# Attention scores in 64-row tiles of the matmul array, instead of from operands stacked by DMA

## The chip, the cores and the metric

The kernel runs on one core of a Trainium2 chip. It is timed in device microseconds (us). The engines are PE (TensorE, matmul; its weight loads are listed apart as PEld), DVE (VectorE), ACT (ScalarE), POOL (GpSimd) and SP (SyncE, here only a DMA queue). Matmul results land in PSUM, eight banks of 128 rows by 512 float32; everything else lies in SBUF.

## The reference

The block is a gated cross-attention followed by a gated top-1 mixture of experts, all in float32: 8 batches of 256 query rows of width 128, 512 context rows each, 16 heads of 64. What matters here is the middle:

```python
xn = _layernorm(x, ln_gamma, ln_beta)            # x is already layer-normed once
q = (xn @ w_q).reshape(B, SQ, NUM_HEADS, DIM_HEAD)
k, v = jnp.split(context @ w_kv, 2, axis=-1)      # then by heads
scores = jnp.einsum('bqhd,bkhd->bhqk', q * SCALE, k)
attn = jax.nn.softmax(scores, axis=-1)
out = jnp.einsum('bhqk,bkhd->bqhd', attn, v).reshape(B, SQ, INNER)
out = (out @ w_out + b_out) * jnp.tanh(gate[0])
```

After it each token picks one of 8 experts by the maximum of its logits, takes a place among at most 160 of that expert, and passes through `relu(x @ w1) @ w2`.

## The kernel before, in words

Every float32 operand of a large product is split in a "hi" and a "lo" part, and a product is three matmuls (hi by hi, lo by hi, hi by lo; `matmul3`). The unit of work is a **pair** of heads: 8 pairs in each of 8 batches, 64 steps in all, which I call slots; `hp` is the pair in the batch, `j` the pair in all. Batches 1 to 6 run in a hardware loop.

In slot `j` the kernel projects keys and queries for pair `j + 4` (`k_project`, `q_project`, PSUM tile `psKQ`); ACT rounds them to hi (`kq_hi`), DVE takes the rest as lo (`kq_lo`), into `HL`, whose upper 64 partitions hold the second head. SP then copies each head's parts by DMA to `ST`, one of four buffers, where one head's hi part lies over its lo part, so that one matmul over all 128 rows forms two of the three products (L400 to L417). A row of minus the maxima rides in the same stack. So a score tile of 128 keys by 256 queries takes two 256-column matmuls (L1106, L1107), 16 a slot, in four steps `c` that alternate between the two banks `psS`.

The maxima for pair `j + 2` come from four 512-column matmuls of hi parts (`max_scores`, L1081, `psM`); DVE reduces them (`row_max`, L802), PE transposes (`max_transpose`, L1091, T below), and ACT writes the row to `ST` (`max_row`). ACT exponentiates the scores to `P32` (L656). DVE and ACT round one head each to float16 (`PHI`; L945, L701), POOL takes the rest (`PLO`, L549). `values` multiplies those of pair `j - 1` with V by 48 matmuls of 65 columns (L1127 to L1129); DVE normalises. One key tile of V is projected a slot (`v_project`, then `v_hi` on ACT and `v_lo` on DVE).

Some slots of a batch carry more: transposes of the attention output and their copy (`o_transposes`, `ot_copy`; hp 0, 1, 4, 6), the output projection (`project`, hp 2), the next context and the token statistics (hp 3), the tokens (`tokens`, hp 4), the choice of experts (`choose`, hp 6) and their places (`place`, hp 7). Each engine runs its list strictly in the order written; semaphores join them. The lists of a slot stand in the `batch` functions.

## Time and profile before

| | |
|---|---|
| median of 3 runs | 570.28 us (567.17 to 572.21) |
| profiled execution | 566.65 us, span 564.9 us |
| mean granted TensorE clock | 0.974 |
| busy share PE / PEld / DVE / ACT / POOL | 89 / 80 / 77 / 68 / 61 % |
| hardware DMA queue, share of 16 engines | 67.2 %, 87.4 MB |

A busy share says how much of the span an engine had an instruction in flight; matmuls overlap their neighbours, so the distance from one start to the next, here called the pitch, tells what one costs in a stream. Of the 87.4 MB, 73.7 are the stacking: 128 transfers of 384 KB and 128 of 192 KB.

### The profile page before, as it was taken

How to read it: one execution, taken by the hardware profiler on the slowest of the kernel's cores; microseconds unless marked ns; L12 is line 12 of the kernel's file. 1: busy time of each engine (PE TensorE's matmuls, PEld its weight loads, DVE VectorE, ACT ScalarE, POOL GpSimd, SP SyncE). 2: the span in 40 equal slices, each digit the busy share in tenths (PEclk: the TensorE clock that was granted, in tenths of full speed). 3: DMA queues.
4: the chain of work that ended last, by engine and by line, in shares of the span. 5: the costliest groups of instructions: out<-in, count | busy, mean ns of one | idle time of the engine just before them, and what ended most of it. 6: DMA issues, size and time to landing. Idle time of an engine off the chain costs nothing.

```text
span 564.9 us, 16275 instructions
## 1 busy us (share of the span) xinstructions
PE 504.8 (89%) x5708; PEld 453.2 (80%) x5708; DVE 437.6 (77%) x814; ACT 382.8 (68%) x671; POOL 343.1 (61%) x210
## 2 busy tenths in 40 slices
PE   4668999999999998999999989999899989986294
PEld 2457889899899887989898979988798979875194
DVE  3579998879987998789878998799869987975112
ACT  3348888768785886688768868687668876872041
POOL 7555579737675666466756666476646664775115
PEclk9879999999999999999999999999999999999599
DMA  7799788957786777577867777577767766850301
GB/s 204 177 238 243 184 212 207 234 116 176 175 204 141 176 167 182 129 175 170 202 146 173 171 174 176 123 174 173 176 143 176 169 141 139 181 148 13 94 10 37
DMA packets 48173, 91.08 MB, mean 161 GB/s; under 512 B 6259, under 2 KB 21027, under 8 KB 48144
## 3 DMA queue, kind: packets, MB, share of 16 engines
q1 hardware_dynamic: 46768, 87.40, 67.2%
q0 software_dynamic: 1376, 3.30, 1.6%
q8 instruction: 18, 0.29, 0.2%
q14 instruction: 11, 0.09, 0.1%
HBM read 10.83 MB, written 5.14 MB: 28 GB/s over the span
## 4 chain that ended last, share of the span: by engine, by line
PE 68%; DVE 11%; issue 7%; ACT 5%; DMA 4%; SPq 2%; POOL 1%; POOLq 0%; DVEq 0%; ACTq 0%
PE psS L1106 9%; PE psM L1081 9%; PE psS L1107 8%; PE psX L1186 4%; PE psO L1127 4%; DVE MX L802 4%; PE psO L1129 4%; PE psKQ L1019 4%; PE psO L1128 4%; PE psKQ L1021 3%; PE psKQ L1020 3%; PE psKQ L1091 2%; PE psX L1139 2%; ACT P L656 2%; PE psX L1020 2%
## 5 line engine op out<-in xcount | busy, mean ns | idle before, releaser
L549 POOL TENSOR_TENSOR PARTS<-P,PARTS 128x1024 f16<-128x1024 f32 x128 | 274.7, 2146 | 163.7 <-ACT PARTS L701 105.4
L656 ACT ACTIVATE P<-psS 128x512 f32<-128x512 f32 x256 | 146.0, 599 | 46.8 <-PE psS L1107 43.2
L802 DVE TENSOR_REDUCE MX<-psM 128x2 f32<-128x1024 f32 x128 | 155.9, 1218 | 11.0 <-PE psM L1081 10.8
L1106 PE MATMUL psS<-ST 128*128 128x256 f32 x512 | 140.8, 302 | 4.0 <-DVE over L896 2.4
L1107 PE MATMUL psS<-ST 128*128 128x256 f32 x512 | 130.2, 282 | 0.0
L1127 PE MATMUL psO<-VH,PARTS 128*128 128x65 f16 x1024 | 106.9, 195 | 2.5 <-POOL PARTS L549 1.6
L1128 PE MATMUL psO<-VL,PARTS 128*128 128x64 f16 x1024 | 105.8, 193 | 0.0
L1129 PE MATMUL psO<-VH,PARTS 128*128 128x65 f16 x1024 | 105.5, 193 | 0.0
L1106 PEld LDWEIGHTS psS<-ST 128*128 128x128 f32 x512 | 97.1, 190 | 9.8 <-issue 6.5
L1107 PEld LDWEIGHTS psS<-ST 128*128 128x128 f32 x512 | 97.5, 190 | 2.4
L1127 PEld LDWEIGHTS psO<-VH,PARTS 128*128 128x128 f16 x1024 | 91.7, 97 | 9.1 <-POOL PARTS L549 2.2
L1129 PEld LDWEIGHTS psO<-VH,PARTS 128*128 128x128 f16 x1024 | 93.6, 97 | 0.0
L1128 PEld LDWEIGHTS psO<-VL,PARTS 128*128 128x128 f16 x1024 | 93.5, 98 | 0.0
L613 ACT ACTIVATE HL<-psKQ 128x768 fp32r<-128x768 f32 x62 | 50.4, 812 | 57.2 <-PE psKQ L1021 53.9
L1081 PE MATMUL psM<-ST 128*128 128x512 f32 x256 | 81.7, 400 | 7.8 <-DMA ST<-HL 5.0
L945 DVE CAST PARTS<-P 128x1024 f16<-128x1024 f32 x64 | 71.3, 1114 | 19.2 <-ACT P L656 16.2
L701 ACT ACTIVATE PARTS<-P 128x1024 f16<-128x1024 f32 x64 | 67.7, 1058 | 5.8
L791 DVE TENSOR_TENSOR VL<-psX,VH 128x512 f16<-128x512 f32 x62 | 42.7, 688 | 20.0 <-ACT VH L631 18.5
L1081 PEld LDWEIGHTS psM<-ST 128*128 128x128 f32 x256 | 43.9, 190 | 14.8 <-issue 4.8
L624 ACT ACTIVATE ST<-psKQ 34x512 fp32r<-34x512 f32 x64 | 38.0, 594 | 14.6 <-PE psKQ L1091 13.3
L783 DVE TENSOR_TENSOR HL<-psKQ,HL 128x512 fp32r<-128x512 f32 x62 | 42.7, 688 | 5.5 <-ACT HL L614 4.3
L631 ACT ACTIVATE VH<-psX 128x512 f16<-128x512 f32 x62 | 36.1, 583 | 2.1 <-PE psX L1021 2.1
(170 smaller groups left out, 850.3 us busy)
## 6 DMA issues: line engine op xcount, KB each, us to landing
ST<-HL SPq DMA_DIRECT2D x128, 384.0 KB, 5.5
ST<-HL SPq DMA_DIRECT2D x128, 192.0 KB, 4.9
ctx_raw<-in_ctx_dram SPq DMA_DIRECT2D x8, 256.0 KB, 4.9
w1s<-in_L_ffn_w_dram SPq DMA_DIRECT2D x8, 256.0 KB, 4.8
w2s<-in_L_ffn_w_dram SPq DMA_DIRECT2D x8, 256.0 KB, 4.5
experts_table<-O POOLq DMA_DIRECT2D x2, 645.0 KB, 6.1
PARTS<-experts_table SPq DMA_DIRECT2D x2, 516.0 KB, 4.2
PARTS<-in_L_xattn_w_kv_dram SPq DMA_DIRECT2D x4, 256.0 KB, 5.1
```

Of the source, the lines that this page charges most:

```text
L549: pool.tensor_tensor(PLO[:, par, h, :], P32[:, h, :], PHI[:, par, h, :], ALU.subtract).then_inc(plo_done, 1)
L613: act.activation(HL[:, hp % 2, H_KHI:H_KHI + KQ], psKQ[:, 0:KQ], ACT.Copy).then_inc(kq_hi_done, 1)
L656: act.activation(P32[:, h, 512 * (c % 2):512 * (c % 2) + 512], psS[c % 2][:], ACT.Exp, scale=SCALE).then_inc(exp_done, 1)
L701: act.activation(PHI[:, hp % 2, 1, :], P32[:, 1, :], ACT.Copy).then_inc(phi1_done, 1)
L802: dve.tensor_reduce(maxima, psM[:], AX.X, ALU.max, negate=True).then_inc(max_done, 1)
L945: dve.tensor_copy(PHI[:, hp % 2, 0, :], P32[:, 0, :]).then_inc(phi0_done, 1)
L1081: last = pe.matmul(psM[:, qt, :], ST[:, buf, h, AQ + P * qt:AQ + P * qt + P], ST[:, buf, h, AK:AQ], start=True, stop=True)
L1106: pe.matmul(dst, ST[:, buf, h, AK + P * kt:AK + P * kt + P], ST[:, buf, h, AQ:STW], start=True, stop=False)
L1107: last = pe.matmul(dst, ST[:, buf, h, BK + P * kt:BK + P * kt + P], ST[:, buf, h, BQ:BK], start=False, stop=True)
L1127: pe.matmul(psO[:, g:g + DH + 1], phi, VH[:, kt, head, 0:DH + 1], start=first_, stop=False)
L1128: pe.matmul(psO[:, g:g + DH], phi, VL[:, kt, head, :], start=False, stop=False)
L1129: last = pe.matmul(psO[:, g:g + DH + 1], plo, VH[:, kt, head, 0:DH + 1], start=False, stop=last_)
```

## The change

Scores and maxima are now made straight from `HL`. The first head's parts lie in partitions 0 to 63, the second's in 64 to 127, and each matmul uses 64 rows of the array; the two heads' matmuls alternate in the program and write different banks. With 64 rows the three products are three matmuls, and minus the maxima come by a fourth, of ones by the row `NM`, 512 columns wide. A slot's scores are thus 4 matmuls of 512 columns and 24 of 256, all of 64 rows, and its maxima 4 of 512 of 64 rows. `ST`, its DMAs and its constants go.

PSUM is dealt anew: `psAB` holds the projection of keys and queries and then scores `c = 0`, `psCD` scores `c = 1` and then the V projection, `psEF` the raw scores for the maxima and then their transposes. The scores of a slot come in two steps of 1024 columns, both heads at once. `AHEAD` falls from 4 to 2, and the maxima are one pair ahead instead of two. `kq_lo` is one instruction of 768 columns instead of two, ACT's extra copy of the queries goes, `P32` and the context parts get a second buffer, the weights' staging gets memory of its own. The batches are written out in the program instead of looped over. In the first batch, two of the x transposes and the statistics of the last ten x tiles are in other slots.

```diff
-    BQ, BK, AK, AQ = 0, SQ, KQ, KQ + SK
-    STW = 2 * KQ
-
-    H_QLO, H_KHI, H_QHI, H_KLO, H_QHI2 = 0, SQ, SQ + SK, 2 * SQ + SK, 2 * KQ
-    HLW = 2 * KQ + SQ
-
-
-    LIFT = 1.875
-    ROW_H, ROW_END = (64, 96), 98
-
-    AHEAD = 4
-    BUFS = AHEAD
+    H_KHI, H_QHI, H_KLO, H_QLO = 0, SK, KQ, KQ + SK
+    HLW = 2 * KQ
+
+
+    LIFT = 7.0
+
+    AHEAD = 2
...
-        P32 = sb("P32", [P, 2, KT * SQ], F32)
+        P32 = sb("P32", [P, 2, 2, KT * SQ], F32)
...
         MX = sb("MX", [P, 2, QT, P], F32)
+        NM = sb("NM", [P, SQ], F32R)
+        ones_r = sb("ones_r", [P, P], F32R)
...
-        psS = [pb(f"psS{i}", [P, 512]) for i in range(2)]
-        psM = pb("psM", [P, QT, 512])
-        psKQ = pb("psKQ", [P, 1024])
+        psAB = pb("psAB", [P, 1024])
+        psCD = pb("psCD", [P, 1024])
+        psEF = pb("psEF", [P, 1024])
         psO = pb("psO", [P, 512])
         psX = pb("psX", [P, 512])
 
@@ -200,9 +195,7 @@
...
-        def kq_banks(j):
-
-            if j in (1, 3):
-                return psS[0][:, 0:SK], psS[1][:, 0:SQ]
-            return psKQ[:, 0:SK], psKQ[:, SK:KQ]
+            return O[:, 1, INNER - n:INNER] if i else P32[:, 0, 0, 0:n]
+
+
+        def kq_bank(j):
+
+            return psCD if j == 1 else psAB
+
+        def score_bank(c):
+
+            return psCD if c else psAB
...
-            def stacks(b, hp):
-
-
-                j = b * PAIRS + hp
-                buf, par = hp % BUFS, hp % 2
-                sp.wait_ge(kq_lo_done, 2 * j + 2)
-                sp.wait_ge(kq_hi_done, 2 * j + 2)
-                if not (is_first(b) and hp < BUFS):
-
-                    sp.wait_ge(score_psum, 4 * j - 4 * (BUFS - 1))
...
-                    if not (is_last(b) and hp + AHEAD >= PAIRS):
-                        stacks(*next_pair(b, hp, AHEAD))
...
                 j = b * PAIRS + hp
-                if not (is_first(b) and hp < 2):
-
-
-                    pe.wait_ge(kq_lo_done, 2 * j - 2 if is_first(b) and hp < AHEAD else 2 * j)
-                if hp == 0:
-                    pe.wait_ge(ctxt_lo_done, b + 1)
+                if j >= AHEAD:
+
+                    pe.wait_ge(exp_done, 2 * (j - AHEAD) + 1)
+                pe.wait_ge(ctxt_lo_done, b + 1)
                 k_cols = slice(INNER + P * hp, INNER + P * hp + P)
-                k_psum, _ = kq_banks(j) if is_first(b) else kq_banks(0)
-                matmul3(k_psum, w_hi[:, k_cols], w_lo[:, k_cols], cT_hi[:], cT_lo[:])
+                matmul3(kq_bank(j)[:, 0:SK], w_hi[:, k_cols], w_lo[:, k_cols], cT_hi[:, b % 2, :], cT_lo[:, b % 2, :])
 
...
-            def max_scores(b, hp, h):
+                matmul3(bank[:], cT_hi[:, b % 2, cs], cT_lo[:, b % 2, cs], w_hi[:, ws], w_lo[:, ws]).then_inc(v_psum, 1)
+
+            def max_scores(b, hp, qt):
+
+
                 j = b * PAIRS + hp
-                buf = hp % BUFS
-                if h == 0:
-                    pe.wait_ge(stack_in[buf], stack_value(b, hp))
-                if not (is_first(b) and hp == 0 and h == 0):
-                    pe.wait_ge(max_done, 2 * j + h)
+                hl = HL[:, hp % 2, :]
+                if qt == 0:
+                    pe.wait_ge(kq_hi_done, j + 1)
+                    if j:
+
+                        pe.wait_ge(mrow_done, j)
+                else:
+                    pe.wait_ge(max_done, 2 * j + 1)
+                for h in range(2):
+                    rows = slice(64 * h, 64 * h + 64)
+                    last = pe.matmul(psEF[:, 512 * h:512 * h + SK], hl[rows, H_QHI + P * qt:H_QHI + P * qt + P],
+                                     hl[rows, H_KHI:H_KHI + SK], start=True, stop=True)
+                last.then_inc(smax_psum, 1)
+
...
+            def scores(b, hp, c):
+
+
                 j = b * PAIRS + hp
-                pe.wait_ge(max_done, 2 * j + 2)
-
-                pe.wait_ge(kq_lo_done, 2 * kq_before)
-                for qt in range(QT):
-                    last = pe.transpose(psKQ[:, KQ + P * qt:KQ + P * qt + P], MX[:, hp % 2, qt, :], ident[:])
-                last.then_inc(mt_psum, 1)
-
-            def scores(b, hp, c):
+                hl = HL[:, hp % 2, :]
+                if c == 0:
+                    pe.wait_ge(mrow_done, j + 1)
+                    pe.wait_ge(kq_lo_done, min(j + 2, B * PAIRS))
+                    if j == 0:
+                        pe.wait_ge(row_consts, 4)
+                    if j + 1 >= B * PAIRS:
+
+                        pe.wait_ge(exp_done, 2 * j - 1)
+                elif j == 0:
+                    pass
+                elif v_group(*back(b, hp, 1)):
+
+                    vb, half, kt = v_group(*back(b, hp, 1))
+                    pe.wait_ge(v_lo_done, vb * 2 * KT + half * KT + kt + 1)
+                else:
+                    pe.wait_ge(exp_done, 2 * j)
+                heads = [(slice(64 * h, 64 * h + 64), score_bank(c)[:, 512 * h:512 * h + 512]) for h in range(2)]
+                for rows, dst in heads:
+                    both = NM[rows, :].unsqueeze(1).to_broadcast([64, 2, SQ])
+                    pe.matmul(dst.rearrange("p (i n) -> p i n", i=2), ones_r[rows, :], both, start=True, stop=False)
+                for i in range(2):
+                    kt = 2 * c + i
+                    for k, q in ((H_KHI, H_QHI), (H_KHI, H_QLO), (H_KLO, H_QHI)):
+                        for rows, dst in heads:
+                            last = pe.matmul(dst[:, SQ * i:SQ * i + SQ], hl[rows, k + P * kt:k + P * kt + P],
+                                             hl[rows, q:q + SQ], start=False, stop=(i == 1 and k == H_KLO))
+                last.then_inc(score_psum, 1)
+
...
+                    if more1:
+                        max_scores(*next_pair(b, hp, 1), 0)
                     scores(b, hp, 0)
                     scores(b, hp, 1)
...
                     if more1:
-                        max_transpose(*next_pair(b, hp, 1), j + AHEAD if ahead else B * PAIRS)
+                        max_scores(*next_pair(b, hp, 1), 1)
...
+                    if j:
+                        values(*back(b, hp, 1))
...
                     if ahead:
+                        if is_first(b) and hp == 2:
+                            pe.wait_ge(w_lo_rest_done, 3)
                         k_project(*next_pair(b, hp, AHEAD))
-                    if more2:
-                        max_scores(*next_pair(b, hp, 2), 0)
-                    if ahead:
                         q_project(*next_pair(b, hp, AHEAD))
+                    if more1:
+                        max_transpose(*next_pair(b, hp, 1))
...
+                    if v_group(b, hp):
+                        if j == 0:
+                            pe.wait_ge(w_lo_rest_done, 3)
+                        v_project(*v_group(b, hp), after_exp=2 * j + 2)
...
-                dve.wait_ge(kq_hi_done, 2 * j + 2)
+                dve.wait_ge(kq_hi_done, j + 1)
                 hl = HL[:, hp % 2, :]
-                k_psum, q_psum = kq_banks(j) if is_first(b) else kq_banks(0)
-                dve.tensor_tensor(hl[:, H_KLO:H_KLO + SK], k_psum,
-                                  hl[:, H_KHI:H_KHI + SK].bitcast(F32), ALU.subtract).then_inc(kq_lo_done, 1)
-                dve.tensor_tensor(hl[:, H_QLO:H_QLO + SQ], q_psum,
-                                  hl[:, H_QHI:H_QHI + SQ].bitcast(F32), ALU.subtract).then_inc(kq_lo_done, 1)
-
-            def v_lo(b, half, kt, bank=psX):
+                dve.tensor_tensor(hl[:, H_KLO:H_KLO + KQ], kq_bank(j)[:, 0:KQ],
...
+                    exps(b, hp, 0)
+                    exps(b, hp, 1)
+                    act.wait_ge(exp_done, 2 * j + 2)
+                    if not (is_first(b) and hp < 2):
+
+                        act.wait_ge(pv_done, j - 1)
+                    act.activation(PHI[:, hp % 2, :, 512:1024], P32[:, hp % 2, :, 512:1024], ACT.Copy)\
+                       .then_inc(phi_done[1], 1)
+                    if not (is_last(b) and hp + AHEAD >= PAIRS):
+                        kq_hi(*next_pair(b, hp, AHEAD))
                     if not (is_last(b) and hp + 1 >= PAIRS):
                         max_row(*next_pair(b, hp, 1))
...
+                    more1 = not (is_last(b) and hp + 1 >= PAIRS)
+                    if more1:
+                        row_max(*next_pair(b, hp, 1), 0)
+                    phi_first(b, hp)
+                    if more1:
+                        row_max(*next_pair(b, hp, 1), 1)
+                    if hp == LOGITS_STEP and not is_first(b):
+
+                        dve.wait_ge(logit_psum, b)
+                    if hp == RANKS_STEP and not is_first(b):
+                        dve.wait_ge(pos_psum, b)
+                    if not (is_first(b) and hp == 0):
+                        normalise_heads(*back(b, hp, 1), is_first(b) and hp == 1)
                     if not (is_last(b) and hp + AHEAD >= PAIRS):
                         kq_lo(*next_pair(b, hp, AHEAD))
```

On PE, first the stretch from the second half of the maxima to the next slot's first scores (`psM` raw scores, `psX` V, `psS` scores), as it was:

```order
L1081 MATMUL psM<-ST 128x512 [waits max_done]
L1081 MATMUL psM<-ST 128x512
L1030 ISA
L1068 REGISTER_ALU [waits ot_done]
L1019 MATMUL psX<-w_hi,cT_hi 128x512 [waits ctxt_lo_done]
L1020 MATMUL psX<-w_lo,cT_hi 128x512
L1021 MATMUL psX<-w_hi,cT_lo 128x512
L1102 ISA [waits mrow_done]
L1106 MATMUL psS<-ST 128x256 [waits exp_done]
L1107 MATMUL psS<-ST 128x256
L1106 MATMUL psS<-ST 128x256
L1107 MATMUL psS<-ST 128x256
```

And the same stretch now, up to the second half of the maxima (V goes to `psCD`, raw scores to `psEF`):

```order
L942 MATMUL psCD<-w_hi,cT_hi 128x512 [waits ctxt_lo_done,exp_done]
L943 MATMUL psCD<-w_lo,cT_hi 128x512
L944 MATMUL psCD<-w_hi,cT_lo 128x512
L1006 MATMUL psEF<-HL 128x512 [waits mrow_done,kq_hi_done]
L1006 MATMUL psEF<-HL 128x512
L1042 MATMUL psAB<-NM,ones_r 128x512 [waits kq_lo_done,mrow_done]
L1042 MATMUL psAB<-NM,ones_r 128x512
L1047 MATMUL psAB<-HL 128x256 x12
L1042 MATMUL psCD<-NM,ones_r 128x512 [waits v_lo_done]
L1042 MATMUL psCD<-NM,ones_r 128x512
L1047 MATMUL psCD<-HL 128x256 x12
L1006 MATMUL psEF<-HL 128x512 [waits max_done]
```

Before, scores waited for the maxima's row and for the exponential that frees their bank. Now the first scores wait for `kq_lo_done`, the lo part of the pair two further, which lies in the same bank, and the second half of the maxima stands in front of everything that follows and waits for DVE.

On DVE, one slot before (`psM` raw scores, `psKQ` keys and queries, `psX` V):

```order
L945 CAST PARTS<-P 128x1024 [waits pv_done]
L796 REGISTER_ALU
L802 TENSOR_REDUCE MX<-psM 128x2 [waits mt_psum,smax_psum]
L780 ISA
L783 TENSOR_TENSOR HL<-psKQ,HL 128x512 [waits kq_hi_done]
L785 TENSOR_TENSOR HL<-psKQ,HL 128x256
L790 REGISTER_ALU
L791 TENSOR_TENSOR VL<-psX,VH 128x512 [waits v_hi_done]
L809 RECIPROCAL rden<-psO 128x4 [waits pv_done]
L813 REGISTER_ALU [waits rden_done]
L817 TENSOR_TENSOR O<-psO,rden 128x2x2x64 [waits ot_psum]
L802 TENSOR_REDUCE MX<-psM 128x2 [waits mt_psum,smax_psum]
```

And one slot now (`psAB` keys and queries, `psCD` V):

```order
L729 TENSOR_REDUCE MX<-psEF 128x2 [waits mt_psum,smax_psum]
L737 CAST PARTS<-P 128x2x512 [waits pv_done,exp_done]
L729 TENSOR_REDUCE MX<-psEF 128x2 [waits mt_psum,smax_psum]
L744 RECIPROCAL rden<-psO 128x4 [waits pv_done]
L752 TENSOR_TENSOR O<-psO,rden 128x2x2x64 [waits ot_psum,rden_done]
L713 TENSOR_TENSOR HL<-psAB,HL 128x768 [waits kq_hi_done]
L719 TENSOR_TENSOR VL<-psCD,VH 128x512 [waits v_hi_done]
L729 TENSOR_REDUCE MX<-psEF 128x2 [waits mt_psum,smax_psum]
```

The two reductions (L729) stood a whole slot ahead of their use; now they are in the slot that uses them, and the first stands behind `v_lo` (L719) of the slot before and whatever else that slot gave DVE at its end.

## Rows read from the trace of the kernel before

**Rows 1.** The page: span, and busy time of each engine.

```profile
span 564.9 us, 16275 instructions
...
PE 504.8 (89%) x5708; PEld 453.2 (80%) x5708; DVE 437.6 (77%) x814; ACT 382.8 (68%) x671; POOL 343.1 (61%) x210
```

**Rows 2.** The page: the chain that ended last, share by engine.

```profile
PE 68%; DVE 11%; issue 7%; ACT 5%; DMA 4%; SPq 2%; POOL 1%; POOLq 0%; DVEq 0%; ACTq 0%
```

**Rows 3.** PE in order of time: start us, duration us, instructions.

```profile
119.68 0.42 PE L1091 MATMUL psKQ<-ident,MX 128*128 128x128 f32 x2
...
282.23 0.42 PE L1091 MATMUL psKQ<-ident,MX 128*128 128x128 f32 x2
...
289.04 0.41 PE L1091 MATMUL psKQ<-ident,MX 128*128 128x128 f32 x2
...
290.82 3.73 PE L1186 MATMUL psX<-wo,OT 128*128 128x128 f32 x32
...
482.04 0.42 PE L1091 MATMUL psKQ<-ident,MX 128*128 128x128 f32 x2
```

**Rows 4.** PE in order of time, within one slot.

```profile
240.36 0.39 PE L1020 MATMUL psKQ<-cT_lo,w_hi 128*128 128x512 f32 x1
240.59 0.39 PE L1021 MATMUL psKQ<-cT_hi,w_lo 128*128 128x512 f32 x1
...
242.81 0.20 PE L1127 MATMUL psO<-VH,PARTS 128*128 128x65 f16 x1
...
243.52 0.20 PE L1129 MATMUL psO<-VH,PARTS 128*128 128x65 f16 x1
243.55 0.36 PE L1106 MATMUL psS<-ST 128*128 128x256 f32 x1
243.75 0.28 PE L1107 MATMUL psS<-ST 128*128 128x256 f32 x1
243.87 0.28 PE L1106 MATMUL psS<-ST 128*128 128x256 f32 x1
```

**Rows 5.** Groups by line: xcount, then busy us, mean ns, idle before.

```profile
L802 DVE TENSOR_REDUCE MX<-psM 128x2 f32<-128x1024 f32 x128 | 155.9, 1218 | 11.0 <-PE psM L1081 10.8
L656 ACT ACTIVATE P<-psS 128x512 f32<-128x512 f32 x256 | 146.0, 599 | 46.8 <-PE psS L1107 43.2
...
L613 ACT ACTIVATE HL<-psKQ 128x768 fp32r<-128x768 f32 x62 | 50.4, 812 | 57.2 <-PE psKQ L1021 53.9
...
L791 DVE TENSOR_TENSOR VL<-psX,VH 128x512 f16<-128x512 f32 x62 | 42.7, 688 | 20.0 <-ACT VH L631 18.5
...
L631 ACT ACTIVATE VH<-psX 128x512 f16<-128x512 f32 x62 | 36.1, 583 | 2.1 <-PE psX L1021 2.1
```

**Rows 6.** ACT in order of time: two exponentials back to back.

```profile
229.42 1.08 ACT L656 ACTIVATE P<-psS 128x512 f32<-128x512 f32 x2
```

**Rows 7.** DVE in order of time: statistics, tokens, choice and places.

```profile
212.86 2.15 DVE L902 TENSOR_TENSOR slot_now<-pos,over 128x2 uint32<-128x2 f32 x1
...
247.20 0.14 DVE L840 COPY mark<-gscale 128x1 f32<-128x1 f32 x1
...
248.38 0.68 DVE L945 CAST PARTS<-P 128x1024 f16<-128x1024 f32 x1
...
254.25 1.58 DVE L853 TENSOR_SCALAR row<-row,mv,rstd 128x128 f32<-128x128 f32 x2
...
265.45 0.16 DVE L864 TENSOR_REDUCE lmax<-psO 128x2 f32<-128x16 f32 x1
...
272.69 0.16 DVE L883 TENSOR_TENSOR rank<-psO,taken 128x16 f32<-128x16 f32 x1
...
274.00 1.23 DVE L802 TENSOR_REDUCE MX<-psM 128x2 f32<-128x1024 f32 x1
```

**Rows 8.** PE's weight loads in order of time: four in a row.

```profile
264.18 0.53 PEld L1154 LDWEIGHTS psO<-gw,tT 128*128 128x128 f32 x4
```

**Rows 9.** PE in order of time: the wait ahead of the first slots.

```profile
22.95 1.05 PE L1081 MATMUL psM<-ST 128*128 128x512 f32 x2 [4.40 <-DMA ST<-HL]
```

More of the change, by code:

```diff
@@ L224, in gated_block @@
         kq_lo_done = sem("kq_lo_done")
-        stack_in = [sem(f"stack_in{i}") for i in range(BUFS)]
         smax_psum = sem("smax_psum")
@@ L231, in gated_block @@
         exp_done = sem("exp_done")
-        phi0_done = sem("phi0_done")
-        phi1_done = sem("phi1_done")
+        phi_done = [sem(f"phi{c}_done") for c in range(2)]
         plo_done = sem("plo_done")
@@ L290, in is_first, with each_batch @@
             return isinstance(b, int) and b == 0
-        def each_batch(eng, body):
-            body(0)
-            with eng.Fori(1, B - 1) as b:
+        def each_batch(body):
+            for b in range(B):
                 body(b)
-            body(B - 1)
-        def stack_value(b, hp):
-            return b * (64 * PAIRS // BUFS) + 64 * (hp // BUFS + 1)
         def v_group(b, hp):
@@ L422, in x1_store @@
                 sp.dma_start(out_b[b], x_now).then_inc(x1_out, 16)
-            for hp in range(AHEAD):
-                stacks(0, hp)
             sp.dma_start(bo[:], b_out.rearrange("(o n) -> o n", o=1).to_broadcast([P, D])).then_inc(bo_in, 16)
@@ L619, in max_row, with v_hi @@
                 act.wait_ge(mt_psum, j + 1)
-                if not (is_first(b) and hp < BUFS):
-                    act.wait_ge(score_psum, 4 * j - 4 * (BUFS - 1))
-                rows = slice(ROW_H[0], ROW_END)
-                act.activation(ST[rows, hp % BUFS, :, BQ:BK],
-                               psKQ[rows, KQ:KQ + SQ].unsqueeze(1).to_broadcast([ROW_END - ROW_H[0], 2, SQ]),
-                               ACT.Copy).then_inc(mrow_done, 1)
-            def v_hi(b, half, kt, bank=psX):
+                act.activation(NM[:], psEF[:, 0:SQ], ACT.Copy).then_inc(mrow_done, 1)
+            def v_hi(b, half, kt, bank=psV):
                 n = b * 2 * KT + half * KT + kt
@@ L707, in batch @@
                         router_exp(b - 1)
-            each_batch(act, batch)
-            ot_copy(B - 1, 3, psS[0])
-            tokt_copy(B - 1, psS[1])
+            each_batch(batch)
+            ot_copy(B - 1, 3, FFN_BANKS[0])
+            tokt_copy(B - 1, FFN_BANKS[1])
             router_exp(B - 1)
@@ L913, in _ @@
             split_w(2)
-            for hp in range(2):
-                kq_lo(0, hp)
-                v_lo(0, 0, hp, V_BANKS[hp])
+            kq_lo(0, 0)
+            dve.wait_ge(row_consts, 1)
+            row_max(0, 0, 0)
+            kq_lo(0, 1)
+            row_max(0, 0, 1)
+            for kt in range(KT):
+                v_lo(0, 0, kt, V_BANKS[kt])
             dve.wait_ge(x_rest_in, 16)
@@ L1316, in rows_out @@
                     s = 2 * i + n
-                    last = pe.transpose(psS[i % 2][:, P * n:P * n + P], yT[:, P * s:P * s + P], ident[:])
+                    last = pe.transpose(FFN_BANKS[i % 2][:, P * n:P * n + P], yT[:, P * s:P * s + P], ident[:])
                 last.then_inc(yrow_psum, 1)
```

368 lines of the change are left out of this document (137 added, 231 removed).

## The prediction, made before the changed kernel ran

> **What bounds the kernel now.** I read the page's busy times first [rows 1]: PE is busy 89% of the span, more than any other. The chain that ended last agrees: 68% of it is PE's [rows 2]. Then PE in order of time, to see what a slot costs. From one maxima transpose to the next, 282.23 to 289.04, an ordinary slot takes 6.81 us; batch 1's first listed transpose (119.68) and batch 7's (482.04) lie six batches apart, so a batch takes 60.4 us [rows 3]. Within a slot the starts follow each other without a hole: a 512-column matmul takes 0.23 us of pitch, a 256-column one 0.12, 24 value matmuls with 23 gaps 0.71, so 0.031 each, and the first float32 matmul after them 0.08 more [rows 4]. PE is fed because work for a pair is made two to four slots ahead. That lead, not PE's work alone, is what the change alters.
>
> **PE's own work.** With the heads side by side at full effect, scores are 2 steps of 0.23 + 6 x 0.12 = 0.95 us, 1.90 a slot against 16 x 0.12 = 1.92 now: no gain. The maxima fall from 4 x 0.23 to 2 x 0.23, a gain of 0.47 a slot, 30 us over 64 slots if PE stayed the bound. Changing between 64 and 128 rows costs something twice a slot, no row shows it. Nothing is the lower end. The upper is 0.3: a matmul lasts 0.28 at a pitch of 0.12, so letting the array run empty exposes 0.16, and a first load and matmul as much again. I take 0.2. Of the page TensorEngine Tiling (Array Packing) in the Trainium skill, the section Key Properties says that changing the tiling mode drains TensorE; by it the lower end would fall away and the sum stay. No row here shows such a change.
>
> **The first loop.** Pair j+2's keys and queries are projected into the bank that the next slot's first scores need. From scores to scores: scores 1.90, second maxima 0.23, mode change 0.2, values 48 x 0.031 + 0.08 = 1.54, keys and queries 3 x 0.23 + 3 x 0.12 = 1.06 and 0.16 until the last has ended [rows 4], `kq_hi` on ACT 0.81 [rows 5], `kq_lo` on DVE. That one is now 768 columns wide; 512 take DVE 0.69 and 768 take ACT 0.81, 1.5 times 0.69 would be 1.03; I take 0.96. Three hand-overs, between nothing and 0.1 each, 0.2 together. Sum **7.06 us**. While kq_hi and kq_lo run, PE has only T, the V projection and the first maxima, about 1.2 us, and then stands still for some 0.8. This eats the 0.47 and more: 7.06 against 6.81.
>
> **The second loop** runs over DVE. The second maxima wait for the first reduction, values, keys and queries stand behind them, and the first reduction stands behind `v_lo`. Reduction 1.22, maxima and mode change 0.43, values 1.54, keys and queries 1.22, kq_hi 0.81, kq_lo 0.96, v_lo 0.69, hand-overs 0.2, less 0.1 for each instruction that starts while the one ahead of it still drains (two of 0.60 take 1.08 together [rows 5, 6]): 6.9, just below the first loop. So all that DVE gets at a slot's end counts nearly in full. In four slots a batch the copy `ot_copy` adds a third way: kq_hi 0.81, the row of maxima (256 columns, 0.35 by those of 512 and 768), ot_copy 0.60 (as wide as an exponential), v_hi 0.58, v_lo 0.69, each less 0.1, and then reduction to queries as before: **7.3**.
>
> **By slot of a batch.** hp 0 and 1: 7.3 each. hp 2: the projection is 3.7 us of PE [rows 3] that fall on PE's own work of about 6.2, with 0.5 of waits for the late v_lo and reduction: 10.4. hp 3: 6.9 plus the context's lo part 0.6 and the statistics, 247.20 to 248.38, 1.2 [rows 7]: 8.7. hp 4: 7.3 plus tokens 1.5: 8.8. hp 5: 7.06 plus copies: 7.4. hp 6: 7.3 plus the choice, five instructions of 0.16 that wait for one another, 0.9: 8.3 with a little cover. hp 7: 6.9 plus places, 272.69 to 274.00, 1.3 or, where its last instruction takes 2.15 instead of 0.16 (212.86, one of five of eight), 3.3; mean 2.5: 9.4. Sum 67.6 against 60.4 (which holds all these extras, mostly covered): **+7.2 a batch, 50 over seven batches**.
>
> The first batch: PE no longer waits 4.40 us for the first stack [rows 9], but two x transposes and the statistics of ten x tiles move into its slots, and these are longer too. I take +5, between -4 and +10. The exponentials, roundings and POOL's part keep their columns, and POOL, at 61%, has room in longer slots. The expert part after the last batch keeps its instructions. The 67% DMA share and ACT's second copy go, worth nothing: neither was waited for in the steady slots.
>
> Sum: +55. The profiled execution took 566.65 us, so 622; the median of the runs shown is 3.6 above it, so I say **625**. Its own range: mode change 0 to 0.3 (-13, +6), hand-overs and kq_lo 0.1 a slot either way (6), first batch (-9, +5): 603 to 642.
>
> **Rivals.**
> *The loads don't run side by side.* Four loads of 128 columns, with matmuls of 8 columns that hide nothing, take 0.53 us for the four, the last 0.19 long: one each 0.113 [rows 8]. Were each of 24 loads of a slot's narrow matmuls to take that in turn, scores are 2.71 + 0.47 = 3.2 instead of 1.9. The first loop becomes 8.3, and only slots that are already longer are spared: 8.3, 8.3, 11.3, 8.8, 8.8, 8.8, 8.4, 9.4, 72.1 a batch, +11.7 x 8: about 664. For it: f32 loads are as dear as 256-column matmuls, and the change has more of them. Against: the heads use different rows. The Trainium skill's page TensorE: Matmul & The Clock Gate, section LDWEIGHTS (loading the stationary operand), says that a load's time follows its columns and not its rows, so halving the rows makes none cheaper; whether two overlap, no row here shows. Chance 0.15.
> *Nothing runs side by side.* Then scores take 4 x 0.23 + 24 x 0.12 = 3.8 and the maxima 0.93 as now; the first loop is 9.2, a batch about 77.5, 17.1 more, and with 8 of them the kernel about 707. Chance 0.08.
> *Faster: PE stays the bound.* The place is kq_hi and kq_lo between the queries and the next scores. If they with their hand-overs took under 1.2 us instead of 2.0, PE's other work would cover them; then a slot is PE's own 6.81 - 0.47 + 0.1, and the kernel about 566.65 - 24, so 546 as a median, if the reductions too come early. For it: 16 busy DMA engines no longer write SBUF, and DVE's cast takes 0.68 at 248.38 [rows 7], when POOL is idle, so an engine's time depends on its neighbours. Against: kq_hi and kq_lo work from PSUM, and to decide it they must shrink by two fifths. Chance 0.08, some of it only part of the way.
> *No net change*: the waits cost just what the maxima save, 0.47 a slot, with DVE's extras covered. Chance 0.05; between this and my forecast lies 0.04.
>
> **How the numbers follow.** The forecast itself has 0.60. The range runs from 590 to 675: it takes in the forecast's own, most of the way down to no change, and the case of loads in turn; outside lie 707 and the fast end, about 0.2. Within 1% is about what a measurement of this kernel can tell from no change. Faster by over 1%: 0.08; within: 0.05; slower: 0.87.
>
> **What would show it.** First, two score matmuls of different heads starting close together, a pair each 0.12 us: else a rival of the loads. Second, on PE a hole of about 0.8 us ahead of the first scores of most slots, released by kq_lo, and one ahead of the second maxima released by the reduction, longest after hp 3, 4, 6 and 7. Third, slots of 7.0 to 7.3 us, hp 2 near 10.4, a batch near 68. PE's busy share should fall though the kernel is longer. I am wrong if PE shows no such holes, or if the batch stays near 60.

## The result: 4.5% slower, half of what was forecast

| | before | after |
|---|---|---|
| median | 570.56 us (567.17 to 572.21, 4 runs) | 595.92 us (594.97 to 596.14, 4 runs) |
| profiled execution, its span | 566.65, 564.9 us | 596.11, 594.1 us |
| one batch, T to T | 60.39 us | 64.53 us |

The ratio is 1.045, interval 1.040 to 1.050. The forecast was 625, between 590 and 675, with 0.87 for slower. Direction and range held; the forecast's 9.6% were twice the real 4.5%.

The page of the changed kernel, span and busy shares, the DMA queue, then the chain that ended last:

```profile
span 594.1 us, 15490 instructions
...
PE 511.3 (86%) x6476; PEld 427.2 (72%) x6476; DVE 394.9 (66%) x750; ACT 349.0 (59%) x477; POOL 326.8 (55%) x208
...
q1 hardware_dynamic: 18096, 11.88, 6.8%
...
PE 56%; DVE 22%; ACT 11%; issue 5%; DMA 2%; POOL 2%; SPq 0%; POOLq 0%; DVEq 0%; ACTq 0%
```

Against [rows 1, 2]: every engine is busy for a smaller share, and in the chain that ended last PE's share fell from 68 to 56%, DVE's rose from 11 to 22% and ACT's from 5 to 11%. No engine is the bound; hand-overs between them are. Groups by line, with idle time before them and its releaser, say which:

```profile
L500 POOL TENSOR_TENSOR PARTS<-P,PARTS 128x1024 f16<-128x1024 f32 x128 | 271.7, 2145 | 178.3 <-DVE PARTS L737 178.2
...
L713 DVE TENSOR_TENSOR HL<-psAB,HL 128x768 fp32r<-128x768 f32 x63 | 60.3, 958 | 84.4 <-ACT HL L555 84.4
...
L555 ACT ACTIVATE HL<-psAB 128x768 fp32r<-128x768 f32 x63 | 51.3, 814 | 82.4 <-PE psAB L944 82.4
...
L1006 PE MATMUL psEF<-HL 64*128 64x512 f32 x256 | 63.3, 487 | 26.8 <-DVE MX L729 21.6
...
L737 DVE CAST PARTS<-P 128x1024 f16<-128x1024 f32 x64 | 47.9, 749 | 14.2 <-ACT P L591 13.8
```

kq_hi waits for the queries and kq_lo for kq_hi, 63 times each: the first loop. The second maxima (L1006) wait 21.6 us for the reduction: the second. kq_lo is 0.96 us as estimated. (The cast's mean of 749 ns is 63 of 0.68 to 0.70 us and one of 4.47, beside two subtractions on POOL in the second slot.) The next view is PE in order of time through a slot of hp 7, from one transpose to the next (8.13 us); a 64-row matmul shows as 64*128:

```profile
286.06 0.38 PE L1015 MATMUL psEF<-ident,MX 128*128 128x128 f32 x2
286.20 0.48 PE L942 MATMUL psCD<-w_hi,cT_hi 128*128 128x512 f32 x1
...
287.49 0.51 PE L1006 MATMUL psEF<-HL 64*128 64x512 f32 x2 [0.34 <-ACT NM L561]
288.21 0.49 PE L1042 MATMUL psAB<-NM,ones_r 64*128 64x512 f32 x2 [0.22 <-DVE HL L713]
288.52 0.90 PE L1047 MATMUL psAB<-HL 64*128 64x256 f32 x12
289.23 0.42 PE L1042 MATMUL psCD<-NM,ones_r 64*128 64x512 f32 x2
...
291.18 0.51 PE L1006 MATMUL psEF<-HL 64*128 64x512 f32 x2 [0.81 <-DVE MX L729]
291.62 0.20 PE L1068 MATMUL psO<-VH,PARTS 128*128 128x65 f16 x1
...
294.19 0.38 PE L1015 MATMUL psEF<-ident,MX 128*128 128x128 f32 x2
```

Twelve narrow matmuls last 0.90 us with 0.28 of the last one's drain in it: 0.62 for 11 gaps, 0.056 each, so 0.113 a pair, as with full overlap. From the first score tile's start to the second's it is 1.02 (288.21 to 289.23), 0.07 over the forecast. The hole ahead of the first scores, released by kq_lo, is there in 54 slots, but of 0.2 us, or 0.5 by the starts (288.21 less 287.49 and 0.23), where 0.8 had been forecast. The hole of 0.81 ahead of the second maxima is released by the reduction. DVE in the same slot (start, duration) shows what held that reduction:

```profile
287.98 0.68 DVE L719 TENSOR_TENSOR VL<-psCD,VH 128x512 f16<-128x512 f32 x1
288.58 0.17 DVE L818 TENSOR_TENSOR rank<-psO,taken 128x16 f32<-128x16 f32 x1
...
289.81 0.16 DVE L837 TENSOR_TENSOR slot_now<-pos,over 128x2 uint32<-128x2 f32 x1
289.90 1.23 DVE L729 TENSOR_REDUCE MX<-psEF 128x2 f32<-128x1024 f32 x1
```

Its maxima were done at 288.00, but v_lo and 12 instructions of `place` stand ahead of it: it starts 1.9 us late. `place` takes 1.3 us here and its last instruction 0.16; in before that one took 1.98 to 2.15 in five of eight batches [rows 7]. POOL at that time, first in before, then in the changed kernel:

```profile
212.85 2.14 POOL L549 TENSOR_TENSOR PARTS<-P,PARTS 128x1024 f16<-128x1024 f32 x1 [1.51 <-ACT PARTS L701]
```
```profile
283.58 4.24 POOL L500 TENSOR_TENSOR PARTS<-P,PARTS 128x1024 f16<-128x1024 f32 x2 [3.66 <-DVE PARTS L737]
290.06 0.19 POOL L485 TENSOR_TENSOR pool_mark<-mhalf 128x1 f32<-128x1 f32 x1 [2.23 <-DVE slot_now L837]
```

In before the last instruction of `place` (212.86 to 215.01) lies beside a subtraction (212.85 to 214.99). In the changed kernel both subtractions have ended at 287.82, ahead of `place`.

Forecast and measured pitch by slot, from the same T rows (batches 1 to 6 agree within 0.02):

| hp | 0 | 1 | 2 | 3 | 4 | 5 | 6 | 7 | batch |
|---|---|---|---|---|---|---|---|---|---|
| forecast | 7.3 | 7.3 | 10.4 | 8.7 | 8.8 | 7.4 | 8.3 | 9.4 | 67.6 |
| after | 7.20 | 7.19 | 10.22 | 8.41 | 7.70 | 7.52 | 8.19 | 8.12 | 64.53 |

### The profile page after: what moved, and what is told of

Its sections match the earlier page's. It is cut to its first block, busy times and chain, and to the rows that moved or that the text cites. A ratio compares the mean times of both kernels' runs of the same rounds, so it can differ in the third digit from the quotient of the medians.

```text
span 594.1 us, 15490 instructions
## 1 busy us (share of the span) xinstructions
PE 511.3 (86%) x6476; PEld 427.2 (72%) x6476; DVE 394.9 (66%) x750; ACT 349.0 (59%) x477; POOL 326.8 (55%) x208
## 4 chain that ended last, share of the span: by engine, by line
PE 56%; DVE 22%; ACT 11%; issue 5%; DMA 2%; POOL 2%; SPq 0%; POOLq 0%; DVEq 0%; ACTq 0%
PE psO L1068 7%; DVE HL L713 6%; ACT HL L555 6%; DVE MX L729 6%; PE psO L1070 5%; PE psO L1069 5%; PE psAB L942 5%; PE psEF L1006 4%; PE psX L1127 4%; PE psCD L1047 4%; PE psAB L944 4%; PE psAB L943 4%; DVE VL L719 4%; PE psAB L1047 3%; PE psAB L1042 2%
## 5 line engine op out<-in xcount | busy, mean ns | idle before, releaser
L729 DVE TENSOR_REDUCE MX<-psEF 128x2 f32<-128x1024 f32 x128 | 156.2, 1221 | 0.5 <-PE psEF L1006 0.5
L713 DVE TENSOR_TENSOR HL<-psAB,HL 128x768 fp32r<-128x768 f32 x63 | 60.3, 958 | 84.4 <-ACT HL L555 84.4
L591 ACT ACTIVATE P<-psAB,lift 128x1024 f32<-128x1024 f32 x64 | 71.3, 1113 | 66.4 <-PE psAB L1047 66.4
L555 ACT ACTIVATE HL<-psAB 128x768 fp32r<-128x768 f32 x63 | 51.3, 814 | 82.4 <-PE psAB L944 82.4
L1006 PE MATMUL psEF<-HL 64*128 64x512 f32 x256 | 63.3, 487 | 26.8 <-DVE MX L729 21.6
L591 ACT ACTIVATE P<-psCD,lift 128x1024 f32<-128x1024 f32 x64 | 70.9, 1108 | 11.3 <-PE psCD L1047 10.3
L1006 PEld LDWEIGHTS psEF<-HL 64*128 64x128 f32 x256 | 24.8, 184 | 57.2 <-DVE MX L729 27.5
L1047 PEld LDWEIGHTS psCD<-HL 64*128 64x128 f32 x768 | 59.0, 188 | 1.1
L1047 PEld LDWEIGHTS psAB<-HL 64*128 64x128 f32 x768 | 57.8, 185 | 1.6
L1047 PE MATMUL psCD<-HL 64*128 64x256 f32 x768 | 58.4, 281 | 0.0
L1047 PE MATMUL psAB<-HL 64*128 64x256 f32 x768 | 57.7, 278 | 0.0
L719 DVE TENSOR_TENSOR VL<-psCD,VH 128x512 f16<-128x512 f32 x60 | 41.3, 689 | 14.6 <-ACT VH L566 14.1
```

What stands on the lines that cost most here:

```text
L555: act.activation(HL[:, hp % 2, H_KHI:H_KHI + KQ], kq_bank(j)[:, 0:KQ], ACT.Copy).then_inc(kq_hi_done, 1)
L591: act.activation(P32[:, hp % 2, :, 512 * c:512 * c + 512], score_bank(c)[:].rearrange("p (h n) -> p h n", h=2), ACT.Exp, bias=lift[:, 0:1] ...
L713: dve.tensor_tensor(hl[:, H_KLO:H_KLO + KQ], kq_bank(j)[:, 0:KQ], hl[:, H_KHI:H_KHI + KQ].bitcast(F32), ALU.subtract).then_inc(kq_lo_done, 1)
L719: dve.tensor_tensor(VL[:, kt, 8 * half:8 * half + 8, :], bank[:].rearrange("p (h d) -> p h d", d=DH), VH[:, kt, 8 * half:8 * half + 8, 0:D ...
L729: dve.tensor_reduce(maxima, psEF2, AX.X, ALU.max, negate=True).then_inc(max_done, 1)
L1006: last = pe.matmul(psEF[:, 512 * h:512 * h + SK], hl[rows, H_QHI + P * qt:H_QHI + P * qt + P], hl[rows, H_KHI:H_KHI + SK], start=True, sto ...
```

## The experiments

Each kernel is the changed one with the edit shown, in the main lines of it. Where a kernel ran only once there is no interval; the verdict then rests on its slots and batches, which repeat from batch to batch within 0.05 us unless the text says otherwise.

### Which path: the projections earlier, or the second maxima later

```diff
 # kq_early: PE
                     if more1:
                         max_scores(*next_pair(b, hp, 1), 1)
+                    if ahead:
+                        k_project(*next_pair(b, hp, AHEAD))
+                        q_project(*next_pair(b, hp, AHEAD))
                     if j:
                         values(*back(b, hp, 1))
 # kq_hi ahead of ACT's rounding of the second half, kq_lo ahead of normalise_heads
```

> The changed kernel, but the keys and queries of pair j+2 are projected right after the second maxima, ahead of the values; ACT rounds them ahead of its half of the exponentials, DVE takes their low part ahead of the normalisation. Theory 1 (the path queries, kq_hi, kq_lo, next scores sets the slot): values of 1.5 us now cover kq_hi and kq_lo; the hole ahead of the first scores goes, a slot falls from 7.2 to about 6.5 and the batch from 64.5 to 59 or less, so 545 to 562 us, faster than the kernel before. Rival (the reductions set the slot: second maxima behind the first reduction): the hole only moves to the second maxima, batch stays within 1.5 us of 64.5, time 584 to 600.

Measured: 590.63 us median, 1.034 of before (1.030 to 1.038). The batch is 64.1, slots 7.14. Missed: the first loop's wait ahead of the scores is gone, but the slot is only 0.06 shorter, because the path V projection, v_hi, v_lo, first reduction, second maxima, which the projections now stand behind, is as long. PE's wait for the reduction grew from 21.6 to 28.2 us. The rival's numbers came true (584 to 600 us, a batch within 1.5 of 64.5).

```diff
 # m1_late: PE
-                    if more1:
-                        max_scores(*next_pair(b, hp, 1), 1)
                     if j:
                         values(*back(b, hp, 1))
+                    if more1:
+                        max_scores(*next_pair(b, hp, 1), 1)
```

> The changed kernel, but the second maxima stand behind the values instead of ahead of them. Nothing on PE waits for the first reduction any more until the values are done. Theory 1 (the path over kq_hi and kq_lo sets most slots, the reduction only those after DVE's extra work): the long slots hp 3, 4, 6 and 7 give back 0.3 to 0.7 us each, but the second reduction and with it the transpose end later; batch 62.5 to 64, time 580 to 592. Rival (the reductions set every slot): 0.5 us or more in every slot, batch 60 or less, time below 567.

Measured: 601.32 us, 1.053 (1.049 to 1.057), slower than the change as it is. Both theories missed. Three of the four long slots fell, as theory 1 said, though by other amounts: hp 3 and 4 from 8.41 and 7.70 to 7.37 and 7.51, hp 6 to 7.64; but the ordinary slots rose from 7.2 to 7.5, hp 7 to 8.9 and hp 2 to 10.65, and the batch stayed at 64.6. The transpose's loads now wait 25.5 us in all for the second reduction, which starts a pass of values later. Each move takes one of two nearly equal paths away and leaves or feeds the other.

### What made DVE's operations long before, and short now

After, tokens take 342 ns each and slot_now 161; before, 803 and 1381 in the mean of the groups. Two things differ: where POOL's subtractions lie, and the DMA traffic. One experiment for each (its waits are left out here):

```diff
 # pool_extra: POOL, behind its subtractions
+                    if hp in (TOK_STEP, RANKS_STEP) and not is_first(b):
+                        pool.tensor_tensor(pool_out[:], wraw[:, 0:1024]..., wraw[:, 1024:2048]..., ALU.subtract)
 # dma_back: SP, in every slot from batch 1 on
+                    for h in range(2):
+                        src = wraw[64 * h:64 * h + 64, 0:2 * KQ]
+                        sp.dma_start(sink[0:64, h, :], src)
+                        sp.dma_start(sink[64:128, h, 0:KQ], src[:, 0:KQ])
```

> The changed kernel with one more subtraction of 128x1024 on POOL, into a tile of its own, behind POOL's work of slots hp 4 and hp 7 of every batch but the first; nothing waits for it. It is there to run beside DVE's tokens (two of 0.34 us) and places. Theory A (a busy POOL is what makes DVE's operations on SBUF alone long): tokens rise from 0.60 for the two to 1.2 or more, the last instruction of places or one of its neighbours from 0.16 to 1 or more, in most batches, and the time rises by 6 to 15 us. Theory B (they were long before because of the stacks' DMA traffic): tokens and places keep 0.60 and 0.16, time within 3 us of 596.

> The changed kernel with the DMA traffic of the kernel before put back: in every slot from batch 1 on, four transfers from SBUF to SBUF with the shapes of the stacks (1.18 MB a slot), from a tile that nobody writes to one that nobody reads; nothing waits for them but the next ones. Theory A (POOL makes the DVE operations long): tokens 0.60 for two, slot_now 0.16, cast 0.69 as without, time within 3 us of 596. Theory B (the DMA traffic makes them long): tokens 1.2 or more for two, cast 1.0 or more, slot_now 1 or more, batch longer by 2 us and more, time above 608.

Measured: pool_extra 621.3 us, dma_back 600.5. The second moved 75.6 MB on the queue, 54.5% of the 16 engines' span (before: 87.4 MB, 67.2%), and the means of these groups are those of the changed kernel to the nanosecond:

```profile
L752 DVE CAST PARTS<-P 128x1024 f16<-128x1024 f32 x64 | 47.9, 749 | 14.2 <-ACT P L606 13.7
...
L803 DVE TENSOR_SCALAR row<-row,mv,rstd 128x128 f32<-128x128 f32 x16 | 4.8, 342 | 0.8 <-POOL rstd L490 0.8
...
L852 DVE TENSOR_TENSOR slot_now<-pos,over 128x2 uint32<-128x2 f32 x8 | 1.3, 161 | 0.3
```

So theory B is out. Its time is 4.6 us over the change as it is, more than the 3 expected, and lies in single slots: one hp 3 of 10.40 instead of 8.41, where PE waits 2.10 us for the next context to land, and four of hp 7 of 8.33 to 8.75, which I did not trace further. In pool_extra, DVE and then POOL around one `tokens`:

```profile
338.46 0.96 DVE L725 TENSOR_TENSOR HL<-psAB,HL 128x768 fp32r<-128x768 f32 x1 [1.34 <-ACT HL L567]
339.72 0.69 DVE L731 TENSOR_TENSOR VL<-psCD,VH 128x512 f16<-128x512 f32 x1 [0.29 <-ACT VH L578]
340.32 1.66 DVE L800 TENSOR_SCALAR row<-row,mv,rstd 128x128 f32<-128x128 f32 x2
341.90 1.21 DVE L741 TENSOR_REDUCE MX<-psEF 128x2 f32<-128x1024 f32 x1
```
```profile
335.04 4.25 POOL L504 TENSOR_TENSOR PARTS<-P,PARTS 128x1024 f16<-128x1024 f32 x2 [1.01 <-DVE PARTS L749]
339.24 2.41 POOL L511 TENSOR_TENSOR pool_out<-wraw 128x1024 f16<-128x1024 f32 x1
```

kq_lo and v_lo, which read PSUM, run beside POOL at 0.96 and 0.69, as ever. Of the tokens, SBUF to SBUF, the first ends with POOL's subtraction (341.65) and the second behind it: 1.66 for the two instead of 0.60. By the starts and ends of all such rows: 0.60 with POOL idle, 1.64 and more in 7 of 7 beside it. In `place` it is not the last instruction that grows but one of its neighbours, the third:

```profile
296.39 1.35 DVE L834 TENSOR_TENSOR rank_hot<-rank,hot_padded 128x16 f32<-128x16 f32 x1
```

The cast takes 0.68 to 0.70 in 63 of 64 cases, here and in the changed kernel, all of them with POOL's subtractions ended or not yet begun; in before 51 of 64 casts overlap one, and their median is 1.27, up to 1.81. Theory A holds for the durations; its time was forecast 6 to 15 us up and is 25 up. The Trainium skill's page SBUF — State Buffer, section SBUF: two separate sides, says that VectorE and GpSimd share one pair of ports as an exclusive lock, which VectorE asks for in a two-port mode or with two SBUF inputs, and that it is the only contention among engines; by that rule the trace agrees.

The batch of pool_extra is 68.3 us and its time 621 us, close to the 67.6 and 625 forecast. hp 4 rose by 1.06 to 8.76 (8.8 forecast), the tokens' own. hp 7 rose by 2.7 to 10.8, past the forecast's 9.4, though `place` grew only by 1.2. Most of what came on top is the clock, in PE's stretches behind the hole (columns: window, us, busy of PE, PEld, DVE, ACT and POOL, granted clock, DMA share, GB/s):

```profile
297.00:299.90 2.90, 0.92 (x16) 0.72 (x12) 2.87 (x12) 2.87 (x3) 1.32 (x3) 1.00 0.00 0
299.90:302.00 2.10, 2.10 (x32) 1.78 (x33) 1.75 (x2) 0.30 (x1) 1.79 (x3) 0.56 0.18 67
302.00:304.00 2.00, 2.00 (x25) 1.87 (x23) 0.61 (x2) 0.00 (x0) 2.00 (x2) 0.61 0.21 74
```

PE stood still for 1.98 us ahead of 299.89, then the granted clock was 0.56 and 0.61 in these windows; the stretch 300.2 to 303.5 alone has 0.50, the lower of the two levels (1.2 of 2.4 GHz). There value matmuls take 0.055 apiece instead of 0.031. So the batch of pool_extra comes near its forecast in part by luck: the clock's loss in hp 7 was in no forecast. In the changed kernel the hole of that slot is 0.81 us and the clock stays 1.00.

### What DVE's extra work costs at a slot's end

```diff
 # extras_late: DVE
                         row_max(*next_pair(b, hp, 1), 0)
+                    if hp == MOMENTS_STEP + 1 and not is_first(b):
+                        token_moments(b - 1)
+                    if hp == TOK_STEP + 1 and not is_first(b):
+                        tokens(b - 1)
                     phi_first(b, hp)
```

> The changed kernel, with nothing moved but token_moments and tokens on DVE: they stand behind the first reduction of the next slot, ahead of the cast, instead of ahead of the reduction. It measures what the reduction's path charges for DVE's extra work. Theory 1 (in the slots of hp 3 and hp 4 the first reduction and with it the second maxima wait for them in full): their pitch falls from 8.41 and 7.70 to 7.6 to 7.8 and 7.1 to 7.3, batch 1.0 to 1.4 us shorter, time 585 to 589. Rival (the reduction is not what these slots wait for): batch within 0.3 us of 64.5, time 592 to 598.

Measured: 586.38 us, batch 63.0, hp 3 at 7.40 and hp 4 at 7.19, all else as it was. Theory 1, a little more than asked for: 1.5 us a batch instead of 1.0 to 1.4, 10 us for four lines moved. The second loop, with all of DVE's extras in it, was described rightly.

### Are the heads side by side, and who sees to it

```diff
 # heads_apart: three matmuls of head 0, three of head 1, again for the other 256 columns
 # heads_far: all seven of head 0, then all seven of head 1
 # one_half: both heads from rows 0 to 63
-                heads = [(slice(64 * h, 64 * h + 64), score_bank(c)[...]) for h in range(2)]
+                heads = [(slice(0, 64), score_bank(c)[...]) for h in range(2)]
```

> The changed kernel, with the score matmuls of each 256-column half in the order three of head 0, then three of head 1, instead of head by head in turn. Work and shapes are the same. Theory 1 (matmuls on different halves of the rows run side by side only where neighbours in the row differ in head; those of one head take 0.113 each in turn): twelve matmuls take 9 steps of 0.113 instead of 6, that is 1.02 instead of 0.68 in pitch, 0.68 a slot more, nearly all on the path: batch 69 to 70, time 628 to 640. Rival (PE takes matmuls of the other head early, past a waiting one): no difference, within 4 us of 596.

> The changed kernel, with all seven matmuls of head 0 for a score tile ahead of all seven of head 1. In turns of three the order made no difference. Theory 1 (PE goes on to a matmul of the other half past waiting ones, at least six of them): no difference, within 4 us of 596, the twelve narrow matmuls still start 0.057 apart. Rival (it looks past three or so): the seven of one head run for the most part alone, 0.23 and 6 x 0.113 = 0.91 of pitch a head, up to 0.7 more for each of two tiles a slot, and the time between 610 and 690.

> The changed kernel, with the scores of both heads computed from rows 0 to 63, so that head 1's are those of head 0: the same number and shapes of matmuls, all on one half of the array's rows. Theory 1 (two matmuls on different halves share a step of 0.113, those of one half take one each): scores take 2 x (0.47 + 1.36) = 3.6 in pitch instead of 1.9, all on the path, batch 14 us longer, time 690 to 710. Rival (a matmul of 64 rows takes half a step by itself and nothing runs side by side): no difference, within 4 us of 596.

Measured: 595.46, 617.48 and 691.61 us. one_half bears out that the halves matter: an ordinary slot takes 8.9 instead of 7.2, as 3.6 for 1.9 asks, though slots with waits absorb a part, so that the batch is 74.5, 10 longer and not 14; three slots of 11.95 with a lower clock bring the time to where it was expected. Twelve narrow matmuls now last 1.60 us:

```profile
296.31 0.70 PE L1042 MATMUL psAB<-NM,ones_r 64*128 64x512 f32 x2 [0.21 <-DVE HL L713]
296.85 1.60 PE L1047 MATMUL psAB<-HL 64*128 64x256 f32 x12
```

That is (1.60 - 0.28) / 11 = 0.12 each; on two halves it is 0.056. So the overlap is real and comes from the halves. heads_apart missed: no difference, where I had expected 9 steps for 6. heads_far came out as its rival said (PE looks past three or so), 0.62 a slot and a time between 610 and 690. PE in order of time there, first score tile:

```profile
290.70 0.46 PE L1042 MATMUL psAB<-NM,ones_r 64*128 64x512 f32 x1 [0.20 <-DVE HL L713]
291.01 0.51 PE L1046 MATMUL psAB<-HL 64*128 64x256 f32 x3
291.25 0.50 PE L1042 MATMUL psAB<-NM,ones_r 64*128 64x512 f32 x1
291.36 0.74 PE L1046 MATMUL psAB<-HL 64*128 64x256 f32 x6
```

In the program head 1's wide matmul (the second L1042) stands behind six narrow ones of head 0; it starts at 291.25 when three of them have. Here, then, PE takes a matmul for the free half past three waiting ones, not past six. The alternation that the change writes out is safe but not needed to that depth. The Trainium skill's page TensorE: Matmul & The Clock Gate, section The mechanism, says that matmuls start and end strictly in program order; this trace differs, and the measurement decides.

### What a change of rows costs

```diff
 # switch64 (switch128: rows 0:128), in values
                 for h in range(2):
+                    if h == 1:
+                        pe.matmul(psO[:, 320:328], ones_r[0:64, :], ones_r[0:64, 0:8], start=True, stop=True)
```

> The changed kernel, with one matmul of 64 rows and 8 columns, into a corner of psO that nobody reads, between the two heads' values in every slot: two more changes between 64 and 128 rows a slot. The changed kernel's rows show 0.43 from the last maxima to the first value matmul, 0.20 above its pitch, and 0.09 from the projections to the maxima. Theory 1 (the change of mode is what costs that): 0.3 to 0.5 us a slot between the heads, nearly all on the path, time 614 to 628. Rival (the 0.20 belongs to the maxima's last matmul and not to the change): 0.1 a slot or less, time below 604.

> The same as switch64, with the added matmul of 8 columns on 128 rows, so that nothing changes between 64 and 128 rows there. It is the control: what is left of the 0.31 us a slot that switch64 added is the matmul's own, with its change from half precision to float32 and back. Theory 1 (the change of mode is dear): 0.1 to 0.15 a slot, batch 65.3 to 65.7, time 602 to 606. Rival (most of it is the float32 matmul among half-precision ones): 0.25 or more a slot, batch 66.5 or more, time 611 to 616.

Measured: 615.18 and 604.03 us; batches 67.0 and 65.5. Eight slots each: +0.31 and +0.12 a slot. The control takes the float32 matmul's own 0.12 away, and by the batches (67.0 less 65.5, over eight) 0.18 is left for the two changes of rows; for the two of the changed kernel's own slot 0.2 had been taken. The Trainium skill's page TensorEngine Tiling (Array Packing), section Key Properties, says that changing the mode drains TensorE; the trace agrees in that two changes cost 0.18 us, and it shows no drain by itself.

### The order that the two paths ask for

Both must run beside the values. `reorder` puts PE's slot as: maxima, scores, second maxima, keys and queries, V projection, transpose, the batch's extra work, values; the V projections one slot later in the table (else v_hi would overwrite values still being read); ACT kq_hi, row of maxima, v_hi, then its rounding; DVE kq_lo, v_lo, then the normalisation. `reorder2` adds extras_late, `reorder3` moves choose and place too:

```diff
 # reorder3: DVE
                         row_max(*next_pair(b, hp, 1), 0)
+                    if hp == LOGITS_STEP + 1 and not is_first(b):
+                        choose(b - 1)
+                    if hp == 0 and b >= 2:
+                        place(b - 2)
                     phi_first(b, hp)
```

> The changed kernel in another order. PE, in a slot: maxima, scores, second maxima, keys and queries of pair j+2, V projection, maxima transpose, the batch's extra work, and the values last; the V projections stand one slot later in the table. ACT rounds kq_hi, the row of maxima and v_hi ahead of its half of the exponentials, DVE does kq_lo and v_lo ahead of the normalisation. So both paths, over kq_hi and kq_lo and over v_hi, v_lo and the first reduction, run beside the values. Theory 1 (these two paths, nearly equally long, set the slots, so that taking away one alone gave 0.05 us): PE becomes the bound, slots of 6.2 to 6.6 us, hp 2 10.0 at most, batch 56 to 59, time 538 to 562, below the kernel before. Rival (what sets the slot is the reductions behind the cast and the exponentials, that is DVE's row from the first scores on): slots stay at 7 or more, batch 62 or more, time above 578.

> The kernel reorder, and token_moments and tokens stand on DVE behind the first reduction of the next slot instead of ahead of it. Theory 1: the second maxima after hp 3 and hp 4 come 0.6 to 1.2 us earlier where DVE's row still sets them; batch 1 to 1.6 us shorter than in reorder, time 7 to 11 us less. Rival (in the new order DVE has slack there): no difference over 2 us.

> The kernel reorder2, with choose and place on DVE also moved behind the first reduction of the next slot, and ACT's exponential of the logits and POOL's scatter a slot later with them. In reorder2 the slots hp 0, 1, 4 and 5 take 6.56 to 6.78 us with PE without a hole, but hp 6 takes 8.46 and hp 7 8.9 to 10.4, because the reduction stands behind choose and place there. Theory 1: both fall to 6.6 to 7.3, batch from 63 to 57.5 to 59.5, time 545 to 562, below the kernel before. Rival (a busy POOL makes place long wherever it stands, and the cast behind it then holds the second reduction): hp 0 or 7 stays above 8.5, batch 60.5 or more, time 568 or more.

Measured: 603.46 us, 1.064 (1.058 to 1.070); 584.50 us, 1.033 (1.028 to 1.039); 562.93 us, 0.994 (0.990 to 0.998). The first missed theory 1, and its rival fits the time and the batch (63.7 to 65.6) but not the ordinary slots. hp 1 and hp 5 take 6.50 to 6.79, PE without a hole, as theory 1 said, and hp 0 6.70 to 7.82; but values now stand directly ahead of the maxima, so normalisation and extras lie between the values and the reduction: hp 3, 4, 6, 7 took 8.0, 8.3, 8.4 and 8.9 to 10.7. reorder2 saved 19 us, twice what was expected (hp 3 to 7.47, hp 4 to 6.76): a part of it is again POOL, beside which the first of two token instructions took 1.70 in reorder and 0.57 in the new place. In reorder3 hp 6 and hp 7 are 7.25 and 7.30, the batch 58.9, PE busy 89%. It is the fastest kernel here: 33 us under the change as it is, and under the kernel before by 0.6% (0.2 to 1.0), too little to count as faster.

## Why the prediction was right in direction and wrong in size

- **PE's own work**: right. Heads fully side by side, no cost of loads, two changes of rows 0.18 (0.2 taken).
- **The first loop**: right in form and size, 7.06 against 7.20; the 0.14 are the two score tiles, 1.02 each instead of 0.95. kq_lo 0.96 as taken. It is not alone: without it a slot takes 7.14.
- **The second loop**: right; moving tokens and moments out of it gave back 1.5 us a batch.
- **The step that failed is the size of DVE's extras in "By slot of a batch"**. Tokens 1.5, places "1.3 or 3.3; mean 2.5": both read from a kernel in which POOL worked beside them, and carried over unchanged. In the changed kernel POOL waits for DVE's cast, does both subtractions in a row (4.25 us) and is idle when DVE comes to its extras (but for the last batch's choice, where `winners` took 2.08 instead of 0.18 beside it): tokens 0.60, places 1.3. hp 4 is 1.1 under the forecast and hp 7 1.3 (tokens 0.9 shorter, places 1.2): 2.4 of the 3.1 us by which the batch was missed; hp 3 gives 0.3 and hp 2 0.2. Over the six batches between the two T that makes 18.4 of the 26 us between 55 forecast and 29 measured, 14.4 of them by hp 4 and hp 7.
- The rest is mostly the end, where the forecast took batch 7 for a batch like the others. For its hp 3 to 7, behind the T at 482.04 in before and 512.36 now, it had +5.8, and the changed kernel is 1.1 shorter there. The last slots did grow, hp 3 to 5 by 2.7 us together; but what follows the last transpose (500.60 and 533.66) shrank by 3.9, which had been put at nothing. No experiment takes that stretch apart.
- The first batch and three slots more, up to the same T (119.68 in before, 125.17): +5.5, where the forecast had 5 and 1.4.
- The prediction had the clue, a cast of 0.68 when POOL is idle, and used it only for the rival that PE stays the bound. It did not ask where POOL's work would lie in the new order. pool_extra shows that this was the cause: with POOL put back beside the extras, hp 4 is at its forecast (8.76 for 8.8).
- Small slips in the sums, none of which decides: 48 values by 0.031 and 0.08 are 1.57, not 1.54; the parts named for the third way add up to 7.1, not 7.3 (hp 0 and 1 took 7.2); and the forecast's own range, added up, starts at 597 and not at 603.
- The rivals: loads in turn and nothing side by side are out (one_half shows what the latter costs: 8.9 a slot). Faster needs both loops gone, and then gave 0.6%.

## What to carry to other kernels

A duration read from a trace belongs to its neighbours there. For a VectorE cast, scalar or two-operand operation from SBUF to SBUF, note what GpSimd did at that moment, and ask where both will be after the change. Where two loops are nearly equally long, an experiment that removes one shows nothing: look for the order that removes both. Work that is off the path should stand behind the reduction that others wait for, and a move that makes values and maxima neighbours moves all of it onto the path again.
